# A decoder layer in one kernel: splits straight from PSUM, fewer stack transfers, self-attention probabilities transposed by DMA, new order

## The reference, cut to what matters

```python
# a: T = 256 tokens, D = 128
q = (x @ Wq.T).reshape(Bv, Tv, H, D)
k = (x @ Wk.T).reshape(Bv, Tv, 1, D) + sinusoidal_pe(1, D)
v = (x @ Wv.T).reshape(Bv, Tv, 1, D)
q = q + sinusoidal_pe(Tv, D)
scores = einsum('bhtd,bsd->bhts', q, k1) / sqrt(D)      # causal mask, softmax
out = einsum('bhtd', probs, v1) @ Wo.T
# b: 16 heads of width 16, keys from ctx
q = query @ Wq.T + bq;  k = key @ Wk.T + bk;  v = value @ Wv.T + bv
scores = q k^T * scale + attn_mask + spatial_bias + directional_bias   # softmax
out = probs v @ Wo.T + bo
# c: gate top-2 of 8, hidden = square(relu(x w1)), out = sum(weight * hidden w2) + shared
```

## Time and profile before

| | |
|---|---|
| time, median of 3 runs (lowest, highest) | 2263.12 us (2261.98, 2266.82) |
| span of the profiled execution | 2269.1 us |
| instructions in the profile | 73067 |
| busy: TensorE, ScalarE, VectorE, GpSimd | 92%, 89%, 82%, 79% |
| moved by DMA | 367.16 MB, mean 162 GB/s |
| mean granted TensorE clock | 0.979 of full speed |

### The profile page before, as it was taken

One profiled execution on the slowest core, in us unless ns is written; L12 is line 12 of the kernel. 1 busy time (PEld: TensorE's weight loads), 2 busy tenths in 40 slices (PEclk: granted clock), 3 DMA queues, 4 the chain that ended last, 5 costly groups with the idle time before them and its releaser, 6 DMA issues.

```text
span 2269.1 us, 73067 instructions
## 1 busy us (share of the span) xinstructions
PE 2080.3 (92%) x24128; PEld 1807.7 (80%) x24128; DVE 1862.2 (82%) x6768; ACT 2024.8 (89%) x5937; POOL 1781.9 (79%) x1899
## 2 busy tenths in 40 slices
PE   4679999999999999999999999999999999999876
PEld 3458888888888888888888888888888888788755
DVE  4578888888888888888888888888888888888863
ACT  5589999999999998999999999999999999899862
POOL 2358888788888877888888888888888888788773
PEclk9789999999999999999999999999999999999998
DMA  4387778688777779776766887777788688788760
GB/s 144 109 182 162 164 164 174 158 170 190 169 158 164 168 155 180 175 160 160 174 167 160 188 180 161 169 164 172 155 183 182 161 160 169 150 164 186 167 135 19
DMA packets 711784, 367.16 MB, mean 162 GB/s; under 512 B 561392, under 2 KB 659952, under 8 KB 711408
## 3 DMA queue, kind: packets, MB, share of 16 engines
q1 hardware_dynamic: 711408, 362.50, 72.8%
HBM read 202.98 MB, written 25.17 MB: 101 GB/s over the span
## 4 chain that ended last, share of the span: by engine, by line
PE 57%; issue 13%; POOL 11%; ACT 8%; DMA 6%; DVE 4%; SPq 1%; ACTq 0%; POOLq 0%; DVEq 0%
PE ps_c_hidden L972 14%; PE ps_c_out L972 13%; PE ps_a_misc L972 13%; DMA b_probsT_hi_lo<-b_probs_hi_lo 5%; PE ps_b_misc L1109 5%; POOL bias L516 3%; PE ps_b_scores L1095 3%; PE ps_a_misc L1051 2%; POOL ctxT_hi L482 2%; ACT c_relu L678 2%; POOL a_qT_lo L474 2%; ACT ps_b_probs L652 2%; POOL ctxT_lo L485 2%; ACT a_qT_hi L597 2%; PE ps_a_scores L1032 1%
## 5 line engine op out<-in xcount | busy, mean ns | idle before, releaser
L516 POOL TENSOR_TENSOR bias<-bias,b_mask 128x512 f32<-128x512 f32 x512 | 644.8, 1274 | 6.2 <-DMA bias<-in_bias 5.8
L832 DVE CUSTOM_DVE_ANT_0 b_neg_scores<-ps_b_scores,bias 128x256 f32<-128x256 f32 x1024 | 391.6, 420 | 70.3 <-POOL bias L516 34.9
L839 DVE TENSOR_TENSOR b_probs_hi_lo<-ps_b_probs,b_probs_hi_lo 128x512 f16<-128x512 f32 x512 | 352.3, 688 | 106.0 <-ACT b_probs_hi_lo L660 103.6
L537 POOL TENSOR_TENSOR c_hidden_lo<-c_hidden,c_hidden_hi 128x512 f16<-128x512 f32 x288 | 335.1, 1164 | 48.4 <-issue 32.7
L972 PE MATMUL ps_c_hidden<-c_xT_hi,w_hi 128*128 128x256 f16 x1152 | 316.8, 275 | 20.2 <-ACT c_relu L678 20.2
L530 POOL TENSOR_TENSOR c_hidden<-c_relu 128x512 f32<-128x512 f32 x288 | 300.2, 1042 | 32.1 <-ACT c_relu L678 12.7
L972 PE MATMUL ps_c_out<-w_hi,c_hidden_hi 128*128 128x256 f16 x1152 | 315.3, 274 | 9.9 <-DVE acc L943 9.9
L972 PE MATMUL ps_c_hidden<-c_xT_lo,w_hi 128*128 128x256 f16 x1152 | 316.3, 275 | 0.0
L972 PE MATMUL ps_c_hidden<-c_xT_hi,w_lo 128*128 128x256 f16 x1152 | 316.3, 275 | 0.0
L972 PE MATMUL ps_c_out<-w_lo,c_hidden_hi 128*128 128x256 f16 x1152 | 315.5, 274 | 0.0
L972 PE MATMUL ps_c_out<-w_hi,c_hidden_lo 128*128 128x256 f16 x1152 | 315.4, 274 | 0.0
(11 more groups left out here) (194 smaller groups left out, 7498.1 us busy)
## 6 DMA issues: line engine op xcount, KB each, us to landing
bias<-in_bias SPq DMA_DIRECT2D x256, 512.0 KB, 4.4
q_stack<-qk_scratch SPq DMA_DIRECT2D x256, 64.0 KB, 2.6
x_ln<-in_x SPq DMA_DIRECT2D x32, 256.0 KB, 4.5
ctxT<-in_ctx SPq DMA_DIRECT2D x32, 256.0 KB, 4.5
x<-in_x SPq DMA_DIRECT2D x32, 256.0 KB, 5.3
qk_scratch<-b_qT_hi_lo SPq DMA_DIRECT2D x32, 256.0 KB, 4.6
qk_scratch<-b_kT_hi_lo SPq DMA_DIRECT2D x32, 256.0 KB, 3.8
k_stack_even<-qk_scratch SPq DMA_DIRECT2D x128, 64.0 KB, 2.5
```

The costliest lines, as they stand in the source:

```text
L516: gp.tensor_tensor(part, part, b_mask[:, :], ALU.add).then_inc(b_c_ok, 1)
L537: gp.tensor_tensor(c_hl[:, u, :], c_h[:, :], c_hh[:, u, :], ALU.subtract).then_inc(c_h_ok, 1)
L832: last = dve.tensor_tensor_reduce(out=b_t[:, u, c, :], in0=ps_bs[:, c * T:(c + 1) * T], in1=bias[:, slot, at:at + T], scale=-2.0, scalar=3 ...
L839: dve.tensor_tensor(b_p2[:, j % DEPTH, :, 1, :], ps_bp[:, :].rearrange("p (c t) -> p c t", c=CT), b_p2[:, j % DEPTH, :, 0, :], ALU.subtrac ...
```

## The change

It has these parts:

- Self-attention q, k and v are split straight from PSUM. ScalarE writes the high part, VectorE the low part by one scalar_tensor_tensor; the fp32 copies in SBUF and the GpSimd subtractions are gone. k and v share one tile (`a_kvh`, `a_kvl`), split by one instruction each. Two banks alternate for q and for `a_pv`: `ps_a_misc` and `ps_a_odd`, the bank that `ps_a_probsT` had.
- The position term of q is not added to q. `a_pk` multiplies the position table (`pe_h`, `pe_l`) by k once for each batch, and VectorE adds the causal mask to it; `a_s` adds the result in place of the mask. The position term of k is a product of a row with ones.
- Cross-attention q, k and v are split in the same way. The biases of q and k are products of a row pair with ones, added in PSUM; the bias of v is carried through Wo once (`b_c0`) and added with `bo`.
- The q and k columns of the weights are permuted, so that the stacks can be stored in 4 transfers each and loaded in 1 (q) and 2 (k), instead of 1 each and 8 each.
- The normalization `a_n` writes an fp16 high part, for heads 0, 2, 4, 6 on GpSimd, for the others on ScalarE; VectorE makes the low part (`a_n_lo`). `a_pT` has both transposed by DMA (768 columns of fp16), into a ring of four; `a_pt` is gone on TensorE, ScalarE and VectorE.
- The weight pieces from the fifth on are loaded by entries `w_load` of SP's list.
- All five lists are new; `LAGS` is 8.

```diff
+POOL_HEADS = [0, 2, 4, 6]
...
+            def w_load(b, n):
+                if isinstance(b, int) and b == 0:
+                    slot = n % SLOTS
                     sp.wait_ge(s_lo, n - SLOTS + 1)
+                    if n < N_PIECES:
+                        a, z = pieces[n]
+                        sp.dma_start(bias[:, slot, 0:z - a], wpair_d[:, a:z]).then_inc(s_stage[slot], 16)
+                    else:
+                        sp.dma_start(bias[:, slot, :], bias_d[n - N_PIECES]).then_inc(s_bias[slot], 16)
...
             def b_store_q(b, _):
-                sp.dma_start(stk_d[0].rearrange("r m p t -> p r m t"), b_q2[:, :, :, :]).then_inc(b_q_dram, 16)
+                for h in range(2):
+                    for u in range(2):
+                        sp.dma_start(stk_d[0, h].rearrange("(u r) d g m t -> u (d g) r (m t)", u=2)[u],
+                                     b_q2[64 * h:64 * h + 64, :, :, :].rearrange("p r m t -> p r (m t)")).then_inc(b_q_dram, 16)
...
             def b_stack_q(b, _):
-                for head in range(2):
-                    for r in range(4):
-                        at = 64 * head + BD * r
-                        sp.dma_start(q_stack[at:at + BD, :, :],
-                                     stacked(0, r // 2, head)).then_inc(b_qst_ok, 16)
+                sp.dma_start(q_stack[:, :, :],
+                             stk_d[0].rearrange("h r d g m t -> (h r d) (g m) t")).then_inc(b_qst_ok, 16)
...
+            def a_pT_load(b, h):
+                head = b * AH + h
+                sp.wait_ge(a_p_ok, head + 1)
+                sp.wait_ge(a_pv_ps, max(head + 1 - A_RING, 0))
+                sp.dma_start_transpose(a_pT[:, head % A_RING, :, :, :].rearrange("p r g t -> p (r g) t"),
+                                       a_p2[:, h % DEPTH, :, :].rearrange("p r t -> p (r t)")).then_inc(
+                                           a_pT_ok[head % A_RING], 16)
...
@block.gpsimd
+            def a_n(b, h):
+                gp.tensor_tensor(a_p2[:, u, 0, 0:128], a_p[:, d, 0:128], a_inv[:, d, 0:1].to_broadcast([P, 128]), ALU.mult)
+                gp.tensor_tensor(a_p2[:, u, 0, 128:384], a_p[:, d, 128:384], a_inv[:, d, 1:2].to_broadcast([P, 256]),
+                                 ALU.mult).then_inc(a_np_ok, 1)
...
@block.vector
+            def a_n_lo(b, h):
+                dve.scalar_tensor_tensor(out=a_p2[:, u, 1, 0:128], in0=a_p[:, d, 0:128], scalar=a_inv[:, d, 0:1],
+                                         in1=a_p2[:, u, 0, 0:128], op0=ALU.mult, op1=ALU.subtract)
+                dve.scalar_tensor_tensor(out=a_p2[:, u, 1, 128:384], in0=a_p[:, d, 128:384], scalar=a_inv[:, d, 1:2],
+                                         in1=a_p2[:, u, 0, 128:384], op0=ALU.mult, op1=ALU.subtract).then_inc(a_p_ok, 1)
+            def a_q_lo(b, r):
+                dve.scalar_tensor_tensor(out=a_ql[:, 2 * r:2 * r + 2, :],
+                                         in0=q_bank[r % 2][:, :].rearrange("p (n t) -> p n t", n=2), scalar=1.0 / W_UP,
+                                         in1=a_qh[:, 2 * r:2 * r + 2, :], op0=ALU.mult,
+                                         op1=ALU.subtract).then_inc(a_ql_ok, 1)
+            def a_pk(b, _):
+                dve.wait_ge(a_pk_ps, after(b, 1, 1))
+                for at in (0, 2 * P):
+                    dve.tensor_tensor(a_tri[:, at:at + P], ps_as[:, at:at + P], tri, ALU.add)
+                dve.tensor_copy(a_tri[:, P:2 * P], ps_as[:, P:2 * P]).then_inc(a_tri_ok, 1)
...
@block.tensor
             def a_qp(b, r):
                 if r == 0:
-                    pe.wait_ge(a_vl_ok, after(b, 1, 1))
+                    pe.wait_ge(a_kvl_ok, after(b, 1, 1))
+                elif r == 1:
+                    pe.wait_ge(a_o_ok, after(b, AH, 0))
                 else:
-                    pe.wait_ge(a_q_ok, after(b, 4, r))
+                    pe.wait_ge(a_ql_ok, after(b, 4, r - 1))
+            def a_pk(b, _):
+                for out, t0, keys in [(ps_as[:, 0:128], 0, P), (ps_as[:, 128:384], P, T)]:
+                    for n, (q, k) in enumerate([(pe_h, a_kvh), (pe_h, a_kvl), (pe_l, a_kvh)]):
+                        last = pe.matmul(out, q[:, t0:t0 + P], k[:, 0:keys], start=(n == 0), stop=(n == 2))
+                last.then_inc(a_pk_ps, 1)
             def b_q(b, _):
                 for m in range(CD):
+                    pe.matmul(ps_c1[:, m * T:(m + 1) * T], b_rows_hl[:, 0, m * P:(m + 1) * P], ones[:, :], start=True,
+                              stop=False)
...
```

479 lines of the change are left out of this document (243 added, 236 removed).

## The result

The changed kernel takes **2374.39 us** (median; 2363.88 to 2384.91), the kernel before 2263.05 on the same chip: a ratio of **1.0489**, 95% interval 1.0465 to 1.0513. It is 4.9% slower. The forecast was 2154, faster, with a range of 2085 to 2245; the time lies outside it, on the side to which 0.14 was given. Four runs of the changed kernel spread by 0.9%; the profiled one is the fastest of them (2363.88).

What follows compares the result with a forecast made beforehand. TensorE (61.2 of 65.9 us a period) and ScalarE (62.6) were taken as tight together. 32 x 62.8 = 2009.6 us, + 160.3 filling and draining, - 10 at the ends, - 6 for the median, gave 2154 us, range 2085 to 2245.

Steps and rivals of the forecast that it cites:

- the price of `a_n_lo`: VectorE's low half of self-attention probabilities: 8 x (0.282 + 0.420) = 5.6 us a period, VectorE 58.4 in all.
- One of the signs that the prediction had set for being wrong: Listed: DMA releasing `a_pv` or `b_pv` mostly, VectorE exceeding 60 us, or period 65 with all engines below 92%.
- Rival 2: DMA transfers or VectorE become the bound, still faster: period 64.5 us, 2208 us in all; chance 0.20.
- TensorE's term: TensorE's own work in a period falls from 61.2 to 59.6 us: 2.6 of transposes gone, 1.0 of products new.
- GpSimd's 51.7: GpSimd's busy time in a period: from 55.4 to 51.7 us, subtractions gone and four `a_n` added.
- ScalarE's 53.6: ScalarE's busy time in a period: from 62.6 to 53.6 us, so that it stops being a bound.
- Its idle time: TensorE's idle time in a period falls from 4.7 to 3.2 us, giving a period of 62.8 us.
- My base period: Period of the kernel before, 65.9 us, from the distance of `a_wo` blocks two iterations apart.
- The DMA term: DMA engine time in a period rises from 47.3 to between 57 and 62 us, 58.5 taken.
- The rival that decides "from a DMA need of 66 us on": Transposes on one in-order queue make it slower: DMA need 68 us a period, 2320 us; chance 0.14.
- The ends: Filling and draining outside the steady periods: 160.3 us before, shortened by 10, bounds 0 to 25.
- The stacks: Cross-attention q and k stack transfers: fewer loads, last stack about 6 us earlier less 2.8, closing TensorE's 1.5 us hole.

Runs made afterwards that it cites:

- Experiments 1: Changed kernel, VectorE's two low-half instructions per head replaced by sums over one SBUF tensor, low half left zero and still transposed: 2221.72 us.
- 8: Not a kernel version: VectorE's two-SBUF-tensor instruction repeated by itself beside one-input and PSUM forms, GpSimd idle, then busy: 0.48 us goes to 0.83.
- 11: Changed kernel, nothing left out, GpSimd's 34 instructions of 128x512 in a period each cut into two of 128x256: 2301.81 us.
- 14: Kernel before, plus two unused VectorE instructions per head (128x128 and 128x256) with two constant SBUF tensors each: 2593.21 us.
- 15: Kernel before, plus two unused VectorE sums per head of 128x128 and 128x256 over one constant SBUF tensor: 2335.61 us.
- experiment 3: Changed kernel, low half replaced by one-input sums, and only the high half transposed (384 columns) and used twice in the product with v: 2210.18 us.
- experiment 9: Changed kernel without the self-attention low half: no VectorE instruction for it, half-width transposes, two products with v instead of three: 2188.35 us.
- experiments 6: Changed kernel's other parts kept, but self-attention probabilities normalised in fp32 and transposed on TensorE as before, in the old order patched: 2431.08 us.
- experiment 2: Changed kernel, low half still computed, but only the high half transposed by DMA (384 columns) and used twice in the product with v: 2379.84 us.

## Why the prediction was wrong

**The step that failed** is the price of `a_n_lo` in the part on VectorE: "The nearest rows for `a_n_lo` read PSUM and it reads SBUF; 15% less would be 57.6, and 10% more on all new work 59.6." The low half took 8 x (0.583 + 0.871) = 11.6 us in place of 5.6. Both ends of that bound were taken from rows of another kind. What mattered was not PSUM or SBUF as such but that both tensor inputs lie in SBUF while GpSimd reads there too, and the step never asked what GpSimd does meanwhile. Experiments 1, 8, 11, 14 and 15 show it from five sides. One of the signs that the prediction had set for being wrong came: VectorE exceeds 60 us (62.8). Rival 2 had named VectorE as the next bound, but even its worst price was 59.6.

Could the trace of before have told it? One line there has two SBUF tensors as inputs at 128x256, the mask of cross-attention (a row not used in the prediction):

```profile
L818 DVE SCALAR_TENSOR_TENSOR b_mask<-key_padding,half_mask x64: 415/418/1377, 87.0 to 2144.4; 128x256 f32<-128x256 uint8 x64
```

Its median says 418 ns; the longest says 1377. It runs at a place where GpSimd has just paused (0.87 us idle before 1017.15 in the iteration around 1016.57), so it is rarely hit: three of the 64 are long, and each begins while a GpSimd instruction of 128x256 or more runs. The longest begins at 2144.40 and ends at 2145.78, and GpSimd's row beside it is

```profile
2144.07 1.42 POOL L537 TENSOR_TENSOR c_hidden_lo<-c_hidden,c_hidden_hi 128x512 f16<-128x512 f32 x1 [0.83 <-issue]
```

which ends at 2145.49, 0.29 us earlier. A mean alone hides that; the spread shows it.

The Trainium skill has the rule, which I did not weigh: "SBUF — State Buffer", section Who interferes with whom, says that a DVE (VectorE) instruction with two SBUF inputs contends with a GpSimd instruction that reads SBUF and not with one that only writes, and that the pair of ports they share is an exclusive lock. Experiment 8 agrees in every form tried, the memset included (475 ns). The page also says that issue order decides who is blocked. The trace of the changed kernel agrees: VectorE's 128x256 instruction takes 1.47 us where GpSimd began first and 0.47 where it began first itself, and then it is GpSimd's that grows, from 1.04 to 1.21 us.

**TensorE's term was right.** Its busy rows give 63.8 us of a period before (1534.95 / 1600 x 66.5) and 61.8 in experiment 1, 2.0 less, forecast 1.6. GpSimd's 51.7 came as 51.3. ScalarE's 53.6 came as 56.6, without effect: it is idle a fifth of the time.

**Its idle time was wrong.** "I take 3.2 us idle: a period of 62.8." In the prices of the prediction (61.2 us of work before, 59.6 after) TensorE idled 66.5 - 61.2 = 5.3 us before, and 65.5 - 59.6 = 5.9 in experiment 1. Relieving ScalarE by 6 us and loading the stacks in fewer transfers did not shrink it, nor did relieving DMA (experiment 3) or VectorE and TensorE together (experiment 9). The rest of the error, 2222 against 2154, is this: 32 x (65.5 - 62.8) = 86 us, less 27 for the ends (123 us where 150 were set), and a median 4 us over the span (2218.2) where 6 under was set: 86 - 27 + 10 = 69. What sets these 5 to 6 us was not isolated; that the in-order lists set them is argued, from experiments 6 and 9, not shown. The clock can be no more than a small part: 20.5 us at half speed between 300 and 1900 us in experiment 1 against 3.4 before are an estimate of up to 0.35 us of a period.

**My base period was a little short.** 65.9 came from two iterations; the mean of 28 is 66.5, and single ones run from 65.6 to 69.9. The ends of the run were overrated by as much, so the sum did not suffer, but the idle time did.

**The DMA term** was low, 64.8 us (0.99 x 65.5) where 57 to 62 was the range. The base of 47.3 is a share of 0.72 of 65.9 us, between 0.70 of one period and 0.728 over the whole span, filling and draining included; in the steady stretch it is 0.77 x 66.5 = 51.2. The added 13.6 lie inside the 9.6 to 12.9 for transposes and 1.8 for stores. The rival that decides "from a DMA need of 66 us on" came close by its condition and still was not what happened: it named the right sign by another cause, so a forecast of "slower" on its account would have been right by luck. Halving a transpose saves (0.99 x 65.5 - 0.89 x 65.2) / 8 = 0.85 us of the engines, and no time at all in experiment 2 and 0.3 us of a period in experiment 3. To issue one takes 1.18 us at 384 columns (experiment 2), 1.22 at 768 and 1.25 at 1024: fixed, as the upper of the two prices had it.

**The ends** gave 29 us in place of 10, beyond the 25 that was my bound (17 in experiment 1). TensorE's long wait for x at the start did not go, though: it is 24.2 us in one piece after, 20.5 before.

**The stacks** do not help: alone they cost 25 us in the old order, and undone in the new one they change nothing that can be told.

## What to carry to other kernels

Before a low half or any other elementwise step moves to VectorE, ask where its tensor inputs lie and what GpSimd does at that time: with both in SBUF and GpSimd already reading, it waited here for the end of GpSimd's instruction, and that wait stands in the profile as busy time. Give it an input in PSUM or one tensor less where that can be done (experiment 8); where it can't, cut GpSimd's instructions shorter (3.1% here, for 5 us more GpSimd work). And look at the least and the longest duration of a row as well as its mean. Of VectorE's groups between 300 and 1900 us of the changed kernel, only these two and a cast of 128x4 have a longest more than 1.3 times their median; a spread like theirs, a factor of three to four, asks for the timeline of the other engines.

## What the runs showed of the hardware that was not expected

- The 128x256 instruction with two SBUF tensors takes 0.47 us alone and 1.47 on average when it begins beside a GpSimd instruction of the changed kernel, most of them 128x512; 0.84 where these are 128x256. It ends 0.28 to 0.29 us after GpSimd's. One with an input in PSUM, or with one SBUF tensor, is unchanged to 0.01 us (experiment 8).
- Where VectorE's begins first, GpSimd's waits: the square of 128x512 takes 1.21 us in place of 1.04.
- GpSimd needs no second tensor for it: scaling one tensor by a constant stretched VectorE's instruction to 0.87 us.
- A DMA share of 0.99 over 1600 us did not bind: taking 10 points off it changed the time by 0.5%.
- VectorE's waits cost clock as well: TensorE stood at half speed for 58.0 us of 1600 in the changed kernel and for 20.5 with VectorE's two instructions replaced (experiment 1).
- Issuing a transpose takes about as long for 384 columns (1.18 us) as for 1024 (1.25).
